# A cross-network tower: the last sum over d in three fp32r passes on split operands, in place of one fp32 matmul

## The reference

```python
x0 = inputs; xk = inputs                      # (b, 39, 16)
for W in filters:                             # f0, f1, f2
    z = jnp.einsum('bfd,bgd->bfgd', x0, xk).reshape(b, f * g, d)
    cur = jnp.einsum('bpd,pm->bmd', z, W)
    outs.append(cur)
    xk = cur
result = jnp.concatenate(outs, axis=1)
return jnp.sum(result, axis=-1)               # then relu(h @ W_top1 + b), relu(.. @ W_top2 + b), @ W_top3
```

## Time and profile before

| | |
|---|---|
| median of 3 runs | 1289.47 us (1288.04 to 1289.68) |
| the profiled execution | 1290.09 us, of which 1288.3 us from its first to its last instruction |
| granted PE clock | 0.999 of full over the span |
| PE, PEld busy | 1246.9 us (97%), 964.5 us (75%) |
| DVE, ACT, POOL busy | 1039.1 us (81%), 749.3 us (58%), 949.5 us (74%) |

### The profile page before, as it was taken

How to read it: one execution, slowest core, us unless ns; L and a number is a source line. 1 busy time by engine, 2 the same in 40 slices (tenths; PEclk the granted TensorE clock), 3 DMA queues, 4 the chain that set the end, 5 groups by cost and what they waited for, 6 DMA issues and landing times.

```text
span 1288.3 us, 19892 instructions
## 1 busy us (share of the span) xinstructions
PE 1246.9 (97%) x5493; PEld 964.5 (75%) x5493; DVE 1039.1 (81%) x3346; ACT 749.3 (58%) x2422; POOL 949.5 (74%) x844
## 2 busy tenths in 40 slices
PE   0799999999999999999999999999999999999999
PEld 0577778777787778777787777877787777877765
DVE  4679886889968997799878998699977999788840
ACT  4456665666646665566656666466655666466641
POOL 6568887788868887688867888588866888675640
PEclk9999999999999999999999999999999999999999
DMA  7632221122222212122211222222121222111000
GB/s 166 170 107 68 68 69 39 51 60 63 64 67 61 54 47 66 49 68 68 69 42 48 63 64 62 66 63 53 46 65 49 68 68 68 46 43 50 1 1 1
DMA packets 121764, 78.69 MB, mean 61 GB/s; under 512 B 77436, under 2 KB 89826, under 8 KB 121652
## 3 DMA queue, kind: packets, MB, share of 16 engines
q1 hardware_dynamic: 106124, 73.45, 20.2%
q0 software_dynamic: 10240, 2.64, 2.3%
q10 hardware_dynamic: 5288, 1.32, 0.5%
HBM read 18.50 MB, written 2.63 MB: 16 GB/s over the span
## 4 chain that ended last, share of the span: by engine, by line
PE 95%; DMA 2%; ACT 1%; SPq 1%; DVE 0%; issue 0%; ACTq 0%; DVEq 0%
PE ps L492 23%; PE ps L496 22%; PE ps L493 22%; PE ps L472 14%; PE ps L517 6%; PE ps L508 5%; PE ps L574 2%; PE ps L584 1%; DMA dense_rows<-in_dense_ctx 1%; DMA w<-in_f 1%; PE ps L455 1%; SPq L359 0%; ACT ps L699 0%; SPq L271 0%; PE ps L591 0%; ACT w_high L701 0%
## 5 line engine op out<-in xcount | busy, mean ns | idle before, releaser
L816 DVE SCALAR_TENSOR_TENSOR terms<-ps,x_scal,terms 128x128 f32<-128x128 f32 x2944 | 807.3, 344 | 162.1 <-ACT terms L661 94.3
L661 ACT ACTIVATE terms<-ps,x_scal 128x128 f32<-128x128 f32 x2048 | 583.5, 368 | 375.8 <-PE ps L496 368.8
L410 POOL TENSOR_TENSOR terms<-terms 128x1024 f32<-128x1024 f32 (+2 forms) x384 | 576.7, 1502 | 186.2 <-DVE terms L816 163.7
L492 PE MATMUL ps<-w_high,x_high 128*128 128x512 f32 (+1 forms) x1280 | 582.9, 455 | 6.4 <-DMA w<-in_f 4.9
L496 PE MATMUL ps<-w_high,x_low 128*128 128x512 f32 (+1 forms) x1280 | 496.7, 388 | 0.0
L493 PE MATMUL ps<-w_low,x_high 128*128 128x512 f32 (+1 forms) x1280 | 494.8, 387 | 0.0
L386 POOL DMA_INDIRECT x_in<-in_tables,row_at x320 | 304.2, 951 | 81.7 <-issue 67.3
L492 PEld LDWEIGHTS ps<-w_high,x_high 128*128 128x128 f32 x1280 | 241.0, 188 | 86.5 <-issue 18.5
L493 PEld LDWEIGHTS ps<-w_low,x_high 128*128 128x128 f32 x1280 | 241.6, 189 | 78.0 <-issue 29.8
L496 PEld LDWEIGHTS ps<-w_high,x_low 128*128 128x128 f32 x1280 | 240.5, 188 | 50.8
L472 PE MATMUL ps<-prods,w 117*128 117x512 f32 x262 | 134.6, 598 | 9.4 <-DVE prods L782 9.4
(11 more groups left out here) (48 smaller groups left out, 412.8 us busy)
## 6 DMA issues: line engine op xcount, KB each, us to landing
prods<-x_cols SPq DMA_DIRECT2D x190, 234.0 KB
x_cols<-x_rows SPq DMA_DIRECT2D x93, 78.0 KB
x_first<-x_cols SPq DMA_DIRECT2D x93, 78.0 KB
x_in<-in_tables,row_at POOLq DMA_INDIRECT x320, 2.4
x_diag<-x_scal SPq DMA_DIRECT2D x256, 9.8 KB
s<-in_f SPq DMA_DIRECT2D x3, 832.0 KB, 11.4
x_rows<-x_in SPq DMA_DIRECT2D x31, 80.0 KB, 2.4
wt<-in_W_top SPq DMA_DIRECT2D x1, 768.0 KB, 12.6
```

Source lines behind the costliest of these rows:

```text
L410: nc.gpsimd.tensor_tensor(t[:, 0:n], t[:, 0:n], t[:, n:2 * n], ALU.add).then_inc(s_tree, 1)
L492: nc.tensor.matmul(y, x1_high[:, par, at:at + P], high, start=True, stop=False)
L661: op = nc.scalar.activation(terms[:, u % 2, FB * ACT_BANKS.index(q) + i, :], ps[:, (BANKS * u + q) % RING, i * G:(i + 1) * G], ACT.Copy, s ...
L816: nc.vector.scalar_tensor_tensor(out=acc, in0=y, scalar=x0, in1=acc, op0=ALU.mult, op1=ALU.add).then_inc(s_mac, 1)
```

## The change

x2 is split into `x2_high` (an fp32r copy) and `x2_low` (the difference), and the scalars x0 likewise before they are laid out; `x0_diag` holds both halves. `sum_s3` becomes three fp32r passes. ACT makes `x2_high` in each step after its bank 0, and DVE makes `x2_low` after its bank 1, by a subtraction of two SBUF operands. ACT stores the scalars twice, DVE subtracts once for each group. The eight SP transfers carry twice the pieces. POOL's last addition waits for DVE's subtraction and no longer for `sum_s3`. The memset of `x0_diag` is twice as large.

```diff
+X2_HIGH, X2_LOW = 0, 1
+SPLIT_SCALARS = (0, 5)
...
-        x0_diag = sb("x0_diag", [P, 2, TILES, TB, FX])
+        x0_hl = sb("x0_hl", [P, 2, TILES, F], F32R)
+        x0_diag = sb("x0_diag", [P, 2, 2, TILES, TB, FX], F32R)
...
+            def put_diag(j):
+                for b in range(TB):
+                    at = slice(b * D, (b + 1) * D)
+                    sp.dma_start(x0_diag[at, j % 2, :, :, b, 0:F].bitcast(F32), x0_hl[at, :, :, :].bitcast(F32)) \
+                        .then_inc(s_diag[j % 2], 16)
...
             def move_diag(gf, j):
-                sp.wait_ge(s_scal, gf + 1)
+                sp.wait_ge(s_scl, gf + 1)
...
-                pool.wait_ge(s_s3, bt * STEPS + u - 1 + CREDIT_S3)
+                if bt * STEPS + u > 1:
+                    pool.wait_ge(s_x2l, bt * STEPS + u - 1)
                 nc.gpsimd.tensor_tensor(x2[:, u % 2], t[:, 0], t[:, 1], ALU.add).then_inc(s_x2, 1)
...
             def sum_s3(bt, u):
-                pe.wait_ge(s_x2, bt * STEPS + u - 1 + CREDIT_X2)
+                pe.wait_ge(s_x2h, bt * STEPS + u - 1)
+                pe.wait_ge(s_x2l, bt * STEPS + u - 1)
...
-                nc.tensor.matmul(ps[:, S3_BANK, 0:TB * FX], x2[:, u % 2, :],
-                                 x0_diag[:, j % 2, t].rearrange("p b f -> p (b f)"),
-                                 start=True, stop=True).then_inc(s_s3, 1)
+                s3_sum = ps[:, S3_BANK, 0:TB * FX]
+                high, low = (x0_diag[:, j % 2, i, t].rearrange("p b f -> p (b f)") for i in range(2))
+                nc.tensor.matmul(s3_sum, x2_high[:, :], high, start=True, stop=False)
+                nc.tensor.matmul(s3_sum, x2_high[:, :], low, start=False, stop=False)
+                nc.tensor.matmul(s3_sum, x2_low[:, :], high, start=False, stop=True).then_inc(s_s3, 1)
...
-                nc.scalar.activation(x0_scal[:, j % 2, :, :],
-                                     ps[:, X1_BANK, 0:TILES * F].rearrange("p (t f) -> p t f", f=F),
-                                     ACT.Copy).then_inc(s_scal, 1)
+                turned = ps[:, X1_BANK, 0:TILES * F].rearrange("p (t f) -> p t f", f=F)
+                if guard:
+                    before = gf - 1
+                    act.wait_ge(s_diag[before % 2], (before // 2 + 1) * (16 * TB))
+                nc.scalar.activation(x0_hl[:, 0, :, :], turned, ACT.Copy).then_inc(s_sch, 1)
+                nc.scalar.activation(x0_scal[:, j % 2, :, :], turned, ACT.Copy).then_inc(s_scal, 1)
...
+            def split_x2_high(bt, u):
+                act.wait_ge(s_x2, bt * STEPS + u - 1 + CREDIT_X2)
+                act.wait_ge(s_s3, bt * STEPS + u - 2 + CREDIT_S3)
+                nc.scalar.activation(x2_high[:, :], x2[:, u % 2, :], ACT.Copy).then_inc(s_x2h, 1)
...
+                    if q == X2_HIGH and u >= 2:
+                        split_x2_high(bt, u)
...
             def tail(bt):
+                split_x2_high(bt, STEPS)
+                split_dense_weights()
                 store_s3(bt, STEPS)
-                split_dense_weights()
-                store_h1(0)
+                store_h1(0, range(3))
+                split_x2_high(bt, STEPS + 1)
+                store_h1(0, range(3, 4))
                 store_s3(bt, STEPS + 1)
...
+            def split_scalars(gf, j):
+                dve.wait_ge(s_sch, gf + 1)
+                dve.wait_ge(s_scal, gf + 1)
+                nc.vector.tensor_tensor(x0_hl[:, 1, :, :], x0_scal[:, j % 2, :, :], x0_hl[:, 0, :, :].bitcast(F32),
+                                        ALU.subtract).then_inc(s_scl, 1)
+
+            def split_x2_low(bt, u):
+                dve.wait_ge(s_x2, bt * STEPS + u - 1 + CREDIT_X2)
+                dve.wait_ge(s_x2h, bt * STEPS + u - 1)
+                nc.vector.tensor_tensor(x2_low[:, :], x2[:, u % 2, :], x2_high[:, :].bitcast(F32),
+                                        ALU.subtract).then_inc(s_x2l, 1)
...
                     if q in DVE_BANKS:
                         mac(bt, u, q)
+                    if q == X2_LOW and u >= 2:
+                        split_x2_low(bt, u)
+                    if front and (tile, q) == SPLIT_SCALARS:
+                        split_scalars(gf, j)
...
             def tail(bt):
+                split_x2_low(bt, STEPS)
                 low = wt1_stack[64:96, :]
...
+                split_x2_low(bt, STEPS + 1)
```

More of the change, by code:

```diff
@@ L149, in cin_tower @@
         x0_scal = sb("x0_scal", [P, 2, TILES, F])
-        x0_diag = sb("x0_diag", [P, 2, TILES, TB, FX])
+        x0_hl = sb("x0_hl", [P, 2, TILES, F], F32R)
+        x0_diag = sb("x0_diag", [P, 2, 2, TILES, TB, FX], F32R)
         terms = sb("terms", [P, 2, TERMS, G])
         x2 = sb("x2", [P, 2, G])
+        x2_high = sb("x2_high", [P, G], F32R)
+        x2_low = sb("x2_low", [P, G], F32R)
         s3 = sb("s3", [P, FX, BATCH])
@@ L207, in cin_tower @@
         s_scal = sem("scalars_stored")
+        s_sch = sem("scalar_highs_ready")
+        s_scl = sem("scalar_lows_ready")
+        s_x2h = sem("x2_high_ready")
+        s_x2l = sem("x2_low_ready")
         s_y = sem("y_bank_ready")
@@ L314, in load_late @@
                 sp.dma_start(bt2[:, :], b_top2[:, :]).then_inc(s_top, 16)
+            def put_diag(j):
[3 more added lines that the diff above has]
+                        .then_inc(s_diag[j % 2], 16)
             def move_diag(gf, j):
-                sp.wait_ge(s_scal, gf + 1)
+                sp.wait_ge(s_scl, gf + 1)
                 sp.wait_ge(s_s3, gf * TILES - TILES + CREDIT_S3)
[L320 to L323, removed]
+                put_diag(j)
             def move_seconds(gf, j):
@@ L354, in _ @@
             move_seconds(1, 1)
[L355 to L359, removed]
+            sp.wait_ge(s_ones, 2)
+            sp.wait_ge(s_scl, 1)
+            put_diag(0)
             load_late()
@@ L732, in step, with store_h1 @@
                     store_r(bt)
-            def store_h1(h):
-                for c, bank in enumerate(L1_BANKS[h]):
+            def store_h1(h, banks=range(H1 // P)):
+                for c in banks:
+                    bank = L1_BANKS[h][c]
                     act.wait_ge(s_h1, 4 * h + c + 1)
@@ L821, in prologue @@
                 nc.vector.memset(wt1_dense[:, :], 0.0).then_inc(s_pad, 1)
-                diag = x0_diag[:, :, :, :, :].rearrange("p a t b f -> p (a t) b f")
-                nc.vector.memset(diag[:, :, :, :], 0.0).then_inc(s_zero, 1)
+                nc.vector.memset(x0_diag[:, :, :, :, :, :].bitcast(F32), 0.0).then_inc(s_zero, 1)
                 dve.wait_ge(s_zero, 1)
                 dve.wait_ge(s_const, 16 * 2)
-                nc.vector.tensor_copy(diag[:, :, :, F], mask[:, :].unsqueeze(1).to_broadcast([P, 2 * TILES, TB])) \
-                    .then_inc(s_ones, 1)
+                for i in range(2):
+                    nc.vector.tensor_copy(x0_diag[:, i, 0, :, :, F], mask[:, :].unsqueeze(1).to_broadcast([P, TILES, TB])) \
+                        .then_inc(s_ones, 1)
                 for c, bank in enumerate(DENSE_BANKS):
@@ L849, in prologue @@
                 split_x1(0, 0)
+                split_scalars(0, 0)
             def step(bt, u, last):
```

## The result

The changed kernel takes 1357.07 us (median of four, 1355.8 to 1357.59); the kernel before took 1289.58 beside it. The ratio is 1.0521, with a 95% interval of 1.0503 to 1.0539. The forecast was 1350, slower. The profiled execution took 1357.59 us, 67.5 more than the profiled one of before, with a span of 1355.8.

A forecast was written before the change was run, and what follows sets the result against it. PE was taken to bound the kernel (95% of the chain). Terms of +53.8, +3.4, +1.1, -0.2, +2.0 and +0.3 gave +60.4 on 1290.09: 1350.5 profiled, 1350 against the median; range 1318 to 1374.

The forecast's parts named there:

- The likeliest case: Whole run: DVE's new subtraction is held by POOL's addition and PE waits; 1350 us, good to 15 either side, chance 0.65.
- 15 plain groups: Groups without `cin3`, neither first nor last: waits of 2.70 less four savings of 0.36, each 2.34 us longer.
- 7 groups with `cin3`: `cin3` in tile 1 lets DVE and POOL catch up; only the first two waits stay, +3.4 us together.
- the last group: Last group of the loop: four steps each wait some 0.36 us, less 0.09 saved; +1.1 us.
- The end: After the loop: `sum_s3` waits for a subtraction that stands behind DVE's last mac; +2.0 us.
- The start: Layout transfers ahead of w2's load carry twice the pieces: +0.3 us taken, +5.5 if issue time doubles; first group's savings -0.2.
- PE's saving: `sum_s3` in each step: three fp32r passes of 0.155 us replace 0.55, saving 0.09 a step, 11.5 us in all.
- The hold: DVE's subtraction starting inside POOL's first addition ends 0.15 us after it; PE waits 0.34, 0.51, 0.72 and 1.13 a group.
- A dearer restart: Rival: the held subtraction starts anew when POOL ends, ending 0.29 us or more after it; 1367 us, chance 0.07.
- The catch-up in tile 3: Tile 3 of a group: DVE, 4.3 us late in all, can recover 4.7, leaving 0.4, just enough.
- half of it: Rival: DVE and POOL settle in another phase, one hold drops out of each group, some 1.3 us each; 1326 us, chance 0.15.
- The clock: Rival: PE's clock falls after waits of 1 us in each group without `cin3`; +32, 1382 us, chance 0.05.

The follow-up runs named there:

- experiment 6: Changed kernel, but in the step with `cin3` ACT stores s3 ahead of product (1, 4)'s high half; DVE's low half one mac later: 1345.92 us, ratio 1.0423.
- experiment 4: Changed kernel without DVE's subtraction for `x2_low`; the third pass reads `x2_high`, and PE and POOL wait for that: 1274.6 us, ratio 0.9887.
- experiment 1: Changed kernel, third pass reading `x2_high`, PE not waiting for `x2_low`, which DVE still makes: 1361.25 us, ratio 1.0559.
- experiment 2: Changed kernel with the subtraction's second operand from PSUM, just ahead of the fourth mac; PE still waits for it: 1277.26 us, ratio 0.9902.
- experiment 3: Changed kernel with x2 split at the end of the step before, DVE's subtraction ahead of POOL's addition; nothing left out: 1276.8 us, ratio 0.9897.
- experiment 5: Kernel before plus one unread DVE subtraction of two SBUF operands behind the fourth mac of each step: 1349.91 us, ratio 1.046.
- experiment 7: Second buffer for x0's halves, added to the changed kernel, 1357.57 us, and to the version of experiment 3, 1277.64 us.

## Why the prediction was right, and what its steps missed

The likeliest case came out: 1357 for 1350, in its own range of 15 to either side, and all the signs named for it are there (1.29 for "near 1.4", 0.15 behind the addition, a pitch of 0.143 for 0.15, a group of 37.56 for 37.6). The lateness of each `sum_s3` against the same one of before gives the terms one by one (groups counted from tile 2 to tile 2):

| term | forecast | measured |
|---|---|---|
| 15 plain groups | 35.1 (2.34 each) | 34.1 (2.27) |
| 7 groups right after those with `cin3` | 16.4 (as plain) | 10.5 (1.50) |
| the first full group | 2.3 (as plain) | 1.7 |
| 7 groups with `cin3` | 3.4 | 15.3 |
| the last group | 1.1 | 1.3 |
| the end | 2.0 | 2.0 |
| the start | 0.1 (+0.3 - 0.2) | 2.7 |
| sum | 60.4 | 67.6 |

That the total is off by only 7 is in part luck: the groups with `cin3` cost 11.9 us more than forecast, and the ones after them 5.9 less. The two do not hang together: with the wait at `cin3` gone (experiment 6) the groups after it still measure 10.6.

- **PE's saving** was 0.12 a step by the rows of `sum_s3` and 0.135 by the plain groups of experiment 4, not 0.09. The pitch of a pass is 0.143, at the lower bound that I had given, and not on the line through 384 and 512 columns. I had read the pitch at 384 from one pair, 0.18; over three passes (623.32 to 623.85) it is 0.177, and the line through that gives 0.15. The issue gap that the Trainium skill gives for a matmul by itself ("TensorE: Matmul & The Clock Gate", Back-to-back issue gap) comes to 0.41 for three, an estimate, and 0.43 was measured: for this size it was nearer than my line. By it the saving is 0.55 - 0.41 = 0.14 a step, 18 us; the 0.13 and 17 of the forecast are a slip.
- **The hold** was right in rule and size. The forecast's waits of 0.34, 0.51, 0.72 and 1.13 were 0.53, 0.39, 0.71 and 1.12, 2.75 for 2.70 together. That DVE's standing and not PE's new dependence is the cause was argued in the forecast; experiments 1, 2, 3 and 5 show it. The Trainium skill states the same condition ("SBUF — State Buffer", Who interferes with whom: two SBUF inputs on VectorE against a GpSimd instruction that reads SBUF; at most one, outside the 2-port modes, does not contend). Experiment 2 agrees, 0.275 against 1.29 us.
- **A dearer restart** did not come. The subtraction ends 0.15 us behind POOL's, where the 115 ns of the Trainium skill ("SBUF — State Buffer", A bandwidth-pool intuition that's wrong), measured there for the other direction, GpSimd held by VectorE, would as an estimate have it at 0.40. The 0.28 us that it takes alone so lie in part inside the wait.
- **The catch-up in tile 3**, forecast as "just enough", was enough: the 15 plain groups are alike within 0.04 us (2.25 to 2.29).
- **`cin3`** is the term that failed. The step says that ACT costs "nothing, while ACT waits for PE and not PE for ACT". I walked DVE's lateness into PE's matmuls alone and not into ACT's queue, where the high half of product (1, 4) stands ahead of the store of s3. With that wait taken away (experiment 6) the seven groups measure 2.8 us together, against 3.4 forecast. DVE's lateness alone makes the wait: experiment 5, without any new copy on ACT, has it too, 11.0 us in seven. The new copies by themselves cost PE little there, 1.2 us in seven waits in experiments 3 and 4, where the kernel before has none.
- **After `cin3`** DVE has caught up, and in the group that follows one subtraction starts when POOL's tree has ended, two start later within its first addition, and one 0.20 us ahead of it (in the first such group 0.28, 0.99, 1.08 and 0.27 us; the last of them starts at 258.52, POOL's addition at 258.72). That comes near the rival "half of it", in seven groups of 32, and they cost 1.50 and not 2.34.

- **The start.** "The wait for the previous group's transfers looks back a whole group. Nothing": true in the loop, wrong for group 1, whose store follows the issue of group 0's transfers at once. But undoing it alone gives nothing back (experiment 7). The transfers' issue did not grow: 5.29 us for eight, 5.46 in the earlier trace rows. What the 2.7 us come from stays open: 0.79 of them are a wait of the first `sum_s3` for `x2_low`, and the rest is no more than executions differ by.
- **The end** is as forecast. PE waits from 1301.9 to 1303.71 for the subtraction behind the last mac.
- **The clock.** In the changed kernel it stayed at its higher level through all waits of 0.8 to 1.8 us (0.997 over the span) and fell only at the start, in a wait of over 4 us. So that rival, which had it fall after waits of 1 us in each plain group, is excluded. The longer waits do not always leave it there: it fell after two of the seven waits of 1.65 us in experiment 1, and after one of 1.84 in experiment 6, where the same wait of 1.83 in the changed kernel left it.

## What to carry to other kernels

Before adding a cheap VectorE instruction, look at where its operands lie and what GpSimd is doing at that moment. With both in SBUF, one that starts inside an addition of GpSimd on SBUF stands until that ends: 0.28 us of work became 1.3 to 1.8, and 126 unread ones cost 59 us; right behind the work that releases GpSimd it was nearly free, as it was with a PSUM operand. When an engine gets late, walk the lateness into every queue that waits for it, ACT's copies among them, and not only into the bound engine.

## What the runs showed of the hardware beyond that

- Whichever starts first goes on, even by little. The low half of a product at 657.69 was 0.22 ahead of POOL's addition of 657.91 and took its 0.68, and POOL's took 2.70 and not 2.40. In the other order, 0.08 behind POOL's start (1303.56, 2.36 long), DVE's instruction on 32x512 took 2.82 and not 0.68, ending 0.54 behind POOL's:

```profile
657.69 0.68 DVE L818 TENSOR_TENSOR prods_low<-prods,prods_high 117x512 fp32r<-117x512 f32 x1
...
1303.64 2.82 DVE L918 TENSOR_TENSOR wt_stack<-wt_dense,wt_stack 32x512 fp32r<-32x512 f32 x1
```

- POOL's gathers are held too, by a DVE subtraction of two SBUF operands that started first. In the loop of the changed kernel 21 gathers start 0.13 to 0.15 us after such a subtraction of 0.68 (as at 653.65) and take 1.36 to 1.38; all the others take 0.94 to 0.97. In experiment 4 seven start 0.27 or 0.28 after it and take 1.22. All of these end 0.82 to 0.84 us after the subtraction. The other way round nothing is held: DVE's low half at 133.93 starts 0.48 into the gather of 133.45, and they take 0.67 and 0.94. The Trainium skill ("SBUF — State Buffer", Who interferes with whom) infers that `tensor_tensor` takes only the read interface of the shared pair and leaves alone the building of a gather's descriptors, which needs the write interface. These rows don't settle that: no run here tells whether it is the descriptors or the reading of the indices that is held:

```profile
653.79 1.37 POOL L397 DMA_INDIRECT x_in<-in_tables,row_at  x1
...
655.47 0.94 POOL L397 DMA_INDIRECT x_in<-in_tables,row_at  x1 [0.30 <-issue]
```
